# Attention weights scaled on VectorE instead of ScalarE, in a windowed-attention and FFN kernel on eight cores

## The reference, cut to what matters

```python
x = x + outer_attn(_layernorm(x), Wq, Wk, Wv, Wo)        # causal, window 256
x = x + ffn_stack(_layernorm(x), Wqkv, ..., W1, b1, W2, b2)

# outer attention, 16 heads of 64
scores = einsum('bhqd,bhkd->bhqk', q, k) * scale + bias
attn = jax.nn.softmax(scores, axis=-1)
out = einsum('bhqk,bhkd->bhqd', attn, v)

# in the stack, DEPTH = 6 times
for i in range(DEPTH):
    x = attn_layer(shift_tokens(x), Wqkv[i], q_scale[i], k_scale[i], Wo[i]) + x
    x = ffn_layer(shift_tokens(x), ln_g[i], ln_b[i], W1[i], b1[i], W2[i], b2[i]) + x

# its attention: windows of 256 queries, each sees its own and the previous window
sim = einsum('bhwie,bhwje->bhwij', bq, bk2) * QK_SCALE
sim = where(mask, -finfo.max, sim)
attn = jax.nn.softmax(sim, -1)
out = einsum('bhwij,bhwje->bhwie', attn, bv2)
```

## Time and profile before

| | |
|---|---|
| median of 2 runs | 18391.5 us (18357.64 to 18425.36) |
| profiled execution, its own time | 18472.98 us |
| span of the slowest core (core 6) in it | 18471.5 us |
| spans of the eight cores | 18088.5 to 18471.5 us |
| DVE busy in the span | 6224.6 us (34%) |
| ACT busy in the span | 3993.7 us (22%) |
| PE busy in the span | 9857.9 us (53%) |

### The profile page before, as it was taken

The page is one execution under the profiler, slowest core; times in us unless marked ns, Lnnn a source line. Parts: engine busy times, 40 slices in busy tenths (PEclk is TensorE's granted clock), DMA queues, the critical chain, the costliest instruction groups (busy, mean ns, idle before and its releaser), DMA issues.

```text
span 18471.5 us, 212968 instructions; the slowest of 8 cores (18088.5 to 18471.5 us)
## 1 busy us (share of the span) xinstructions
PE 9857.9 (53%) x50402; PEld 4877.9 (26%) x50720; DVE 6224.6 (34%) x22182; ACT 3993.7 (22%) x12412; POOL 1841.4 (10%) x3920
## 2 busy tenths in 40 slices
PE   5554444565444475444575444575444476444576
PEld 3221323222223132222122222122222122322123
DVE  4334434323333313333313333313333312333322
ACT  1221232201323201323101323201223200222200
POOL 0000101001111001111001111001111000101000
PEclk7565555598555587555577555577555577555577
DMA  1001000021000010000110000010000010000011
GB/s 47 20 18 36 23 19 22 10 58 27 19 22 18 25 47 26 17 25 16 30 41 25 18 24 17 27 43 25 19 22 18 23 45 25 21 21 19 10 48 62
DMA packets 761723, 496.57 MB, mean 27 GB/s; under 512 B 77001, under 2 KB 728778, under 8 KB 759512
## 3 DMA queue, kind: packets, MB, share of 16 engines
q1 hardware_dynamic: 760542, 482.93, 9.2%
HBM read 466.09 MB, written 16.78 MB: 26 GB/s over the span
## 4 chain that ended last, share of the span: by engine, by line
PE 44%; DVE 19%; issue 16%; ACT 12%; POOL 5%; DMA 3%; DVEq 1%; ACTq 1%; POOLq 0%; SPq 0%; PEldq 0%
ACT s_pbuf L816 5%; DVE s_ptb L872 4%; PE psB L1140 3%; PE psA L1140 3%; PE psC L1146 3%; PE psG L1146 3%; PE psB L1182 3%; PE psA L1182 3%; DVE s_ssb L658 2%; DVE s_act L1162 2%; ACT s_ggel L1155 2%; DVE s_t1b L697 2%; PE psA L615 2%; POOL s_sqb L653 2%; PE psE L895 2%
## 5 line engine op out<-in xcount | busy, mean ns | idle before, releaser
L823 DVE RECIPROCAL s_rrec<-s_rsum 128x1 f32<-128x1 f32 x1792 | 293.8, 164 | 4018.0 <-ACT s_pbuf L816 4018.0
L730 PE MATMUL psC<-s_ident,s_qpp 128*128 128x128 bf16 x768 | 211.8, 276 | 2393.1 <-DVE s_qpp L718 2393.1
L830 ACT ACTIVATE s_pnorm<-s_pbuf,s_rrec 128x384 bf16<-128x384 bf16 (+2 forms) x1792 | 1066.3, 595 | 974.6 <-DVE s_rrec L823 936.0
L863 PE MATMUL psG<-s_ident,s_pnorm 128*128 128x128 bf16 x2520 | 725.0, 288 | 995.4 <-DVE s_ptb L872 991.3
L863 PE MATMUL psH<-s_ident,s_pnorm 128*128 128x128 bf16 x2520 | 727.5, 289 | 940.4 <-DVE s_ptb L872 934.7
L615 PE MATMUL psA<-s_wbf,s_xn 128*128 128x128 bf16 x4608 | 514.8, 280 | 1127.3 <-POOL s_wbf L602 1126.0
L669 ACT ACTIVATE s_nmax<-s_rnb 128x2 f32<-128x2 f32 x1536 | 312.4, 203 | 3495.5 <-POOL s_rnb L664 3495.5
L658 DVE TENSOR_REDUCE s_ssb<-s_sqb 128x2 f32<-128x128 f32 x1536 | 431.2, 281 | 1564.0 <-POOL s_sqb L653 1562.2
L1140 PE MATMUL psA<-s_xn,s_w1abf 128*128 128x512 bf16 (+1 forms) x2028 | 638.3, 467 | 543.1 <-DVE s_act L1162 259.0
L1140 PE MATMUL psB<-s_xn,s_w1abf 128*128 128x512 bf16 (+1 forms) x2052 | 640.6, 462 | 508.2 <-DVE s_act L1162 501.8
L872 DVE CAST s_ptb<-psG 128x128 bf16<-128x128 f32 x2520 | 726.0, 288 | 289.1 <-PE psG L863 249.7
(11 more groups left out here) (255 smaller groups left out, 19744.9 us busy)
## 6 DMA issues: line engine op xcount, KB each, us to landing
s_wland<-fwqkv SPq DMA_DIRECT2D x288, 512.0 KB, 4.0
s_w1land<-fw SPq DMA_DIRECT2D x252, 512.0 KB, 5.2
s_w2land<-fw SPq DMA_DIRECT2D x126, 512.0 KB, 6.1
s_woland<-fwo SPq DMA_DIRECT2D x96, 512.0 KB, 4.3
s_xland<-x SPq DMA_DIRECT2D x16, 512.0 KB, 4.1
s_woland<-wq SPq DMA_DIRECT2D x16, 512.0 KB, 3.9
s_woland<-wk SPq DMA_DIRECT2D x16, 512.0 KB, 3.8
s_woland<-wv SPq DMA_DIRECT2D x16, 512.0 KB, 3.8
```

The costliest lines, as they stand in the source:

```text
L830: B.emit("S", lambda e, r=r, s3=s % 4, ncols=ncols: e.activation(out=sb[f"pnorm{s3}"][:, 0:ncols], in_=sb[f"pbuf{s3}"][:, 0:ncols], func=A ...
L863: B.emit("T", lambda e, s3=s3, jj=jj, bk=bk: e.matmul(out=bk[:, 0:128], lhsT=sb[f"pnorm{s3}"][:, 128 * jj:128 * (jj + 1)], rhs=I16(), star ...
```

## The change

The multiplication of `pbuf` by the reciprocal is moved from ScalarE (an ACTIVATE with function Copy and a scale for each partition) to VectorE (a `tensor_scalar` with one multiplication and the same scale for each partition), directly behind the reciprocal. VectorE now waits on its own counter between the two, since the second reads what the first wrote. The wait for the transposes that read this `pnorm` buffer last moves to VectorE, ahead of the reciprocal, in place of the wait for ScalarE's last reading of `rrec`. The transposes wait for VectorE's counter instead of ScalarE's.

```diff
@@ emit_sim
         B.wait("V", "S", stok)
-        B.wait("V", "S", st["rrec_war"].get(r, 0))
+        B.wait("V", "T", st["pnorm_war"].get(s % 4, 0))
         B.emit("V", lambda e, r=r: e.reciprocal(
             out=sb["rrec"][:, r:r + 1], in_=sb["rsum"][:, r:r + 1]), inc="V")
         st["rsum_war"][r] = B.tok("V")
-        vt = B.tok("V")
-        B.wait("S", "V", vt)
-        B.wait("S", "T", st["pnorm_war"].get(s % 4, 0))
-        B.wait("S", "S", war_sim.get(("S", s % 4), 0))
-        B.emit("S", lambda e, r=r, s3=s % 4, ncols=ncols: e.activation(
-            out=sb[f"pnorm{s3}"][:, 0:ncols], in_=sb[f"pbuf{s3}"][:, 0:ncols],
-            func=AF.Copy, scale=sb["rrec"][:, r:r + 1]), inc="S")
-        st["rrec_war"][r] = B.tok("S")
-        sim_info[s] = (B.tok("S"), ncols)
+        rv = B.tok("V")
+        B.wait("V", "V", rv)
+        B.emit("V", lambda e, r=r, s3=s % 4, ncols=ncols: e.tensor_scalar(
+            out=sb[f"pnorm{s3}"][:, 0:ncols], in0=sb[f"pbuf{s3}"][:, 0:ncols],
+            scalar1=sb["rrec"][:, r:r + 1], scalar2=None, op0=ALU.mult), inc="V")
+        sim_info[s] = (B.tok("V"), ncols)
@@ emit_tail
-        B.wait("T", "S", norm_tok)
+        B.wait("T", "V", norm_tok)
```

## The result

The changed kernel takes 18784.67 us (median of 11 runs, 18609.17 to 19136.36) against 18325.56 us before (median of 10). The ratio is 1.0227, with a 95% interval of 1.0153 to 1.03: slower, by 2.3%. Ratios and their intervals here leave out the executions in which the cores of one half of the chip ran at a lower clock, medians do not. Since the interval begins at 1.5%, the times do not settle whether the loss is over 2%. The forecast was 18870 us in a range of 18710 to 19060, and 479 us more than before; the medians are 459 us apart.

A forecast was written before the change was run, and what follows sets the result against it. The prediction took attention's loop of waits (scores, exp, reciprocal, block copy, transpose) as the bound, no engine being near full. Added DVE work of 508 us less 29 gave 479, on 18391.5 us: 18870 us, range 18710 to 19060.

The forecast's parts named there:

- The bound: In attention, each step's loop runs scores, exp, reciprocal, block copy, transpose; anything put between reciprocal and copy lengthens it.
- What the removal is worth: 1792 ScalarE multiplications, 1066.3 us, leave ACT: worth nothing in 384-column steps, -29 us where ACT is in the loop.
- the first windows: Steps with fewer columns, where exp stands behind ACT's old multiplication: 0.3 us less a pair, -29 us in all.
- the exchanged wait ahead of the reciprocal: On DVE, TensorE's counter replaces ScalarE's; already met, it costs what the old one cost, a queue entry.
- The multiplication's length: The new tensor_scalar on DVE takes 312 ns at 384 columns: 253 as a copy plus 59 for the pointer.
- the copy rows: Profile rows of bf16 SBUF copies, 220 ns at 256 columns and 420 at 1024, giving 0.26 ns a column.
- rival A: DVE multiplication slower per column: half the copy's rate gives 19030 us, the one-column rate 19330 us; chance 0.15.
- the pointer operand: Operand of the DVE multiplication that comes from a pointer; claimed to add 59 ns, taken from the LayerNorm's tensor_scalar.
- The wait and the handover: On DVE, multiplication 0.26 us behind the reciprocal's start, block copy 0.23 later; loop longer by 0.32 us a step.
- The LayerNorm's 0.10 us: DVE's wait for its own conversion in a LayerNorm, some 0.10 us after its end, taken for the new wait.
- Rival B: DVE's wait on itself is free: loop grows by 0.22 us, 18714 us, inside 2%; chance 0.13.
- The sum: In attention, 1568 full steps at 0.324 us give 508 us, less 29 for steps with fewer columns: 479 us.

The follow-up runs named there:

- experiment 8: Changed kernel with the multiplication moved behind the next tail's first block copy; first to last reciprocal, summed over 14 attn_loop runs: 5620 us.
- experiment 2: Kernel before without ScalarE's multiplication and its wait, weights not normalized; first to last reciprocal, summed over 14 attn_loop runs: 5488 us against 5701.
- experiment 6: Changed kernel without the redundant TensorE wait ahead of the reciprocal; first to last reciprocal, summed over 14 attn_loop runs: 6037 us, -116.
- experiment 1: Kernel before plus only VectorE's wait for its own reciprocal ahead of the first block copy; reciprocal span summed over 14 attn_loop runs: 6093 us, +392.

## Why the prediction was right

*The bound.* Right. The loop ran through reciprocal, first copy and transpose, and experiment 8 shows it in the most direct way: the same work, with its wait, behind the copy instead of ahead of it gives back the whole loss.

*What the removal is worth.* Right for full steps, which gain nothing that can be told from ScalarE's relief (experiment 2), and for the first windows, which gain 0.35 us a pair (forecast 0.3). I left out the first steps of each run, see the sum below. I had costed the exchanged wait ahead of the reciprocal at what the old one cost; experiment 6 shows that each such entry costs 0.065 us, so "the same as before" was the right answer for a wait that is not free.

*The multiplication's length.* Forecast 312 ns, measured 320 for 384 columns; the group's mean of 314 covers smaller forms too. With the forms kept apart (count, busy time, mean ns):

```profile
L828 DVE TENSOR_SCALAR s_pnorm<-s_pbuf,s_rrec 128x384 bf16<-128x384 bf16 x1568 | 502.1, 320 | 175.3 <-DVE s_rrec L823 10.7
L828 DVE TENSOR_SCALAR s_pnorm<-s_pbuf,s_rrec 128x256 bf16<-128x256 bf16 x112 | 32.0, 286 | 12.3 <-DVE s_rrec L823 0.5
L828 DVE TENSOR_SCALAR s_pnorm<-s_pbuf,s_rrec 128x128 bf16<-128x128 bf16 x112 | 28.5, 255 | 12.4 <-DVE s_rrec L823 0.5
```

That is 65 ns for 256 columns more, 0.25 ns a column, about the 0.26 of the copy rows, so rival A is out. Against the 253 ns that those rows give for a copy of 384 columns the pointer operand costs 67 ns rather than 59 (at 256 columns 286 against 220 ns). The Trainium skill's rule in "VectorE: DVE Perf Modes", "The perf-mode tier table", that `tensor_scalar` goes at a copy's rate, agrees with this slope.

*The wait and the handover.* Right in this kernel, and not to be carried over to another. The multiplication starts 0.27 us behind the reciprocal (forecast 0.26), the copy 0.235 behind the multiplication (forecast 0.23), and the loop is longer by 0.34 us (forecast 0.32). But the two terms are not the prices of two things that could be had singly. By them the wait alone would cost 0.16 + 0.10 - 0.17 = 0.09 us a step, and that is what I expected of experiment 1. It costs 0.23, and the multiplication behind it adds only 0.10 to that. The LayerNorm's 0.10 us was not at fault, it is also the time from the reciprocal's end to the multiplication. What I had not counted were the copy's own two waits, which cost 0.13 us more where they stand directly behind the wait, and nothing behind the multiplication. Had the change been only the wait, I would have been 242 us short. It was luck, not insight, that the change had something long enough to stand in front of them.

*Rival B.* Refuted. The multiplication starts 0.27 us behind the reciprocal and not 0.16, and in experiment 1 the wait took the first copy from 0.17 to 0.40 us. The Trainium skill, "VectorE: DVE Perf Modes", "The DRAIN you can't avoid", reports that eight copies took the same time with a semaphore after each as with one after the last, and that the semaphore cost nothing extra there. For the short reciprocal of this kernel that does not hold.

*The sum.* Forecast 508 - 29 = 479, measured +453. A second half grew by 38.4 us where 41 was forecast. The rest is at the start of each run: the first steps have no block copy behind them, and the reciprocals there came closer together than before. First two reciprocals of that stretch in the kernel before, then two in the changed one:

```profile
3118.92 0.16 DVE L823 RECIPROCAL s_rrec<-s_rsum 128x1 f32<-128x1 f32 x1 [1.33 <-ACT s_pbuf L816]
3120.41 0.16 DVE L823 RECIPROCAL s_rrec<-s_rsum 128x1 f32<-128x1 f32 x1 [1.33 <-ACT s_pbuf L816]
```

```profile
3218.40 0.16 DVE L823 RECIPROCAL s_rrec<-s_rsum 128x1 f32<-128x1 f32 x1 [31.86 <-ACT s_pbuf L816]
...
3218.94 0.16 DVE L823 RECIPROCAL s_rrec<-s_rsum 128x1 f32<-128x1 f32 x1
```

They are 0.54 us apart instead of 1.49, because exp stood behind the old multiplication there. The forecast put this at nothing. The first three distances shrank by 2.3 us together, while the ordinary ones grew by 0.33 each. A first half grew by 24 us in the inner layers, forecast 26, and by 39 in the outer one, where the forecast counted 31 and set the small steps to zero. The forecast also gave a chance of 0.85 to a loss of over 2%; on that the interval of 1.5 to 3.0% does not decide.

## What to carry to other kernels

On an engine that works its list in order, the place of an instruction matters more than the engine's load: find the instruction for which another engine waits, and put nothing new ahead of it. The same multiplication, with its wait, cost 453 us ahead of the copy and nothing one place later. Count the waits as well as the instructions. A wait that is already met costs about 0.07 us where nothing, or only a 0.16 us reciprocal, is at work in front of it, so redundant ones are worth looking for there; behind the 0.32 us multiplication taking one out gave nothing. And when an engine at 22% is relieved of a quarter of its work, little follows unless some other engine was waiting for that work; here only the first windows and the first steps of each run gained.

## What the runs showed of the hardware that was not expected

A wait of an engine for its own short instruction can cost more than the time to its end, because the waits queued behind it come only afterwards: the copy's start moved from 0.17 to 0.40 us. The new start is made of the reciprocal (0.17), 0.10 us until its wait is through, and 0.13 us for two further waits, long met, that were handled while the reciprocal ran in the kernel before.

The part of the kernel outside attention varies nearly as much as the effect under study. In one execution of the changed kernel two cores had the same attention sum (6154.6 and 6151.7 us) and spans 334 us apart, at a different mean clock:

```profile
core 1: 18734.0 us, clock 0.637
...
core 4: 18400.0 us, clock 0.653
```

The sum over the stage in question repeats within some 3 us, where the times alone tell only an interval of 1.5 to 3.0%.
